# The turn of a deformable-convolution kernel: ScalarE issues half of the box rows and takes the first units in another order

## What is computed

```python
x = x + _L0_conv_ref(_gn(x), ...)      # attention, 8 heads of 48
x = x + _L1_conv_ref(_gn(x), ...)
# inside _L1_conv_ref:
offset = jnp.clip(_conv(x, off_w, off_b), -max_off, max_off)
mask = 2.0 * jax.nn.sigmoid(_conv(x, mask_w, mask_b))
y = _deform_conv(x, offset, mask, proj_w, proj_b)   # 9 taps, bilinear, 384 -> 384
yn = (y - mean) * rsqrt(var + 1e-05) * gamma + beta # mean, var over the batch
return gelu(yn)
```

## Time and profile before

| | |
|---|---|
| median of 3 runs | 3217.5 us (3216.02 to 3220.64) |
| the profiled execution | 3215.74 us |
| its span (first to last instruction) | 3213.9 us |
| PE / DVE / ACT / POOL busy | 2853.9 / 2057.6 / 1638.9 / 900.9 us |
| DMA | 327.84 MB, mean 102 GB/s |

### The profile page before, as it was taken

The page is one execution under the profiler, slowest core; times in us unless marked ns, Lnnn a source line. Parts: engine busy times, 40 slices in busy tenths (PEclk is TensorE's granted clock), DMA queues, the critical chain, the costliest instruction groups (busy, mean ns, idle before and its releaser), DMA issues.

```text
span 3213.9 us, 80068 instructions
## 1 busy us (share of the span) xinstructions
PE 2853.9 (89%) x32858; PEld 1660.8 (52%) x32858; DVE 2057.6 (64%) x3435; ACT 1638.9 (51%) x2828; POOL 900.9 (28%) x633
## 2 busy tenths in 40 slices
PE   4897999979999799989999799997999989995693
PEld 2454555545555455545555455554555545562461
DVE  5774677746776477855777467674677647773234
ACT  4363544645455553745537354465546555372554
POOL 0351113611153110821127111361116311171110
PEclk9899999989999899999999899998999989997796
DMA  4003551055410652126520455105531065304658
GB/s 143 21 2 104 147 132 57 2 144 150 105 43 22 170 136 78 37 75 159 139 69 3 116 147 128 51 2 146 154 99 42 29 149 135 90 21 164 192 148 326
DMA packets 176190, 327.84 MB, mean 102 GB/s; under 512 B 21036, under 2 KB 101036, under 8 KB 168960
## 3 DMA queue, kind: packets, MB, share of 16 engines
q1 hardware_dynamic: 75760, 182.90, 22.1%
q10 hardware_dynamic: 98400, 126.45, 12.9%
q0 software_dynamic: 1584, 12.58, 0.9%
HBM read 227.58 MB, written 75.27 MB: 94 GB/s over the span
## 4 chain that ended last, share of the span: by engine, by line
PE 38%; issue 20%; POOL 15%; DMA 10%; ACT 6%; DVE 5%; SPq 3%; ACTq 2%; POOLq 0%; DVEq 0%
PE R L1797 14%; POOL PL L810 14%; PE R L1773 7%; PE G L1559 5%; DMA P<-positions_scratch 4%; PE G L1592 3%; DMA hats_scratch<-MHL 3%; PE R L1637 3%; SPq L722 2%; ACTq L1109 2%; PE R L1714 2%; ACT HYB L1081 2%; DVE MXP L1289 1%; DMA positions_scratch<-XP 1%; PE R L1655 1%
## 5 line engine op out<-in xcount | busy, mean ns | idle before, releaser
L1797 PE MATMUL R<-P,WALL 128*128 128x512 f16 x3888 | 937.4, 379 | 7.1 <-issue 7.1
L1289 DVE TENSOR_REDUCE MXP<-G 128x1 f32<-128x512 f32 x997 | 656.2, 686 | 301.4 <-PE G L1592 299.8
L810 POOL TENSOR_TENSOR PL<-P 128x1024 f16<-128x1024 f32 x263 | 600.4, 2288 | 624.8 <-ACT P L989 623.3
L989 ACT ACTIVATE P<-R 128x1024 f32<-128x1024 f32 x512 | 519.6, 1022 | 222.9 <-PE R L1637 222.6
L1797 PEld LDWEIGHTS R<-P,WALL 128*128 128x128 f16 x3888 | 369.5, 97 | 426.5 <-issue 8.1
L1361 DVE TENSOR_TENSOR PL<-P 128x1024 f16<-128x1024 f32 x249 | 457.5, 1842 | 97.9 <-ACT P L989 97.5
L834 POOL TENSOR_TENSOR MHL<-M,MHL 128x504 f16<-128x504 f32 (+1 forms) x144 | 168.1, 1167 | 1114.0 <-ACT MHL L1093 1114.0
L1637 PE MATMUL R<-QK 48*128 48x512 f16 (+1 forms) x3072 | 427.9, 384 | 21.3 <-ACT P L989 12.5
L1655 PEld LDWEIGHTS R<-VS,P 128*128 128x128 bf16 x4096 | 322.7, 97 | 187.4 <-issue 129.6
L1592 PE MATMUL G<-QK,QZ 112*128 112x512 f16 x997 | 378.5, 386 | 22.0 <-DVE MXP L1289 20.0
L1655 PE MATMUL R<-VS,P 128*128 128x49 f16 x4096 | 373.0, 186 | 9.7 <-DVE PL L1361 7.2
(11 more groups left out here) (147 smaller groups left out, 3018.7 us busy)
## 6 DMA issues: line engine op xcount, KB each, us to landing
P<-positions_scratch SPq DMA_DIRECT2D x288, 256.0 KB, 4.3
PM<-positions_scratch SPq DMA_DIRECT2D x144, 256.0 KB, 4.6
XB<-hats_scratch ACTq DMA_DIRECT2D x144, 133.0 KB
XB<-hats_scratch ACTq DMA_DIRECT2D x144, 129.5 KB
XB<-hats_scratch ACTq DMA_DIRECT2D x144, 126.0 KB
hats_scratch<-MHL ACTq DMA_DIRECT2D x48, 266.0 KB
hats_scratch<-MHL ACTq DMA_DIRECT2D x48, 259.0 KB
X<-x SPq DMA_DIRECT2D x8, 1536.0 KB, 7.7
```

The costliest lines, as they stand in the source:

```text
L810: pool.tensor_tensor(PL[:, s % P_BUFS, :], P32[:, s % P_BUFS, :], high_view(s), ALU.subtract).then_inc(p_low_pool, 1)
L989: act.activation(P32[:, s % P_BUFS, :], ST[s % 2], ACT.Exp, scale=SCALE).then_inc(p_exp, 1)
L1289: dve.reduce_max(MXP[:, name[1] % 2, n // 2, n % 2:n % 2 + 1], chunk(sec, name)[:, :], AX.X).then_inc(dve_read, 1)
L1797: last = pe.matmul(R6[:, CT + ct, :], WALL[:, w:w + 128], PHL[:, u % 2, part // 2, t, :], start=(u % TAPS == 0 and n < CT), stop=(u % TAPS ...
```

## The change

- `AHEAD` becomes 2: products and fp16 copies are made two units ahead.
- ACT issues the six box row transfers of q = 2 and 3, right behind the mask; SP issues the other six as before and no longer has any between unit 0's and unit 1's rows.
- ACT's turn is written out anew: after unit 0's fp16 copy it reads one fill and stores unit 0, and the x hats of unit 1 come behind that; then load of unit 0, fill, y hats of unit 1, fill, its fp16 copy, x hats of unit 2, store of unit 1, v piece 5, the copy of the sampled unit 0, load of unit 1, y hats of unit 2. v pieces 3 and 4 stand before and between unit 0's hats.
- DVE reads v pieces 3 and 4 before the first product, three fills before the second, and makes the remainder of the sampled unit 0 before the third.

```diff
-UNIT_COUNT, T_RING, AHEAD = 4, 2, 3
+UNIT_COUNT, T_RING, AHEAD = 4, 2, 2
...
# sync
                 for u in range(UNITS):
                     spread(units_0, out_0, u)
-                    if u == 0:
-                        boxes_out(range(2, PER_BLOCK))
...
# scalar, behind the mask (MSK)
                 act.wait_ge(act_read, sec.at(("comb",), "A"))
+                act.wait_ge(xt_low, b * 16 + 16)
+                for q in (2, 3):
+                    for part, a in ((0, 0), (1, 1), (2, 0)):
+                        act.dma_start(box_rows(q, part), transposed_rows(q, a)).then_inc(xt_in[q], 16)
...
# scalar, taps
+                    def sample_high(u):
+                        act.wait_ge(sampled, m_0 + (u + 1) * UNIT_COUNT)
+                        for t in range(CT):
+                            act.activation(PHL[:, u % 2, 0, t, :], R6[:, t, :], ACT.Copy).then_inc(p_hi, 1)
+                    if not final:
+                        v_halves(3)
                     hats_x(0)
+                    if not final:
+                        v_halves(4)
                     hats_y(0)
                     m_halves(0, 0)
-                    if not final:
-                        v_halves(3)
-                        v_halves(4)
+                    next_fill()
+                    store_m(0, 0)
+                    next_fill()
                     if reach == NEAR_OFF:
                         hats_x(1)
-                    for q in range(PER_BLOCK):
-                        act.wait_ge(xt_in[q], b * 48 + 48)
-                    for n in range(AHEAD):
-                        here, after = [divmod(k, per_unit(reach)) for k in (n, n + 1)]
-                        if n < T_RING:
-                            store_m(*here)
-                        if reach == NEAR_OFF:
-                            if n > 0:
-                                hats_x(n + 1)
-                            hats_y(n + 1)
-                        next_fill()
-                        if n < T_RING:
-                            load_boxes(*here)
-                        if n + 1 < AHEAD:
-                            m_halves(*after)
-                    while fills:
+                        boxes_landed()
+                        load_boxes(0, 0)
                         next_fill()
+                        hats_y(1)
+                        next_fill()
+                        m_halves(1, 0)
+                        hats_x(2)
+                        store_m(1, 0)
+                        if not final:
+                            v_halves(5)
+                        sample_high(0)
+                        load_boxes(1, 0)
+                        hats_y(2)
...
-                            if c == per_unit(reach) - 1:
-                                for t in range(CT):
-                                    act.activation(PHL[:, u % 2, 0, t, :], R6[:, t, :], ACT.Copy).then_inc(p_hi, 1)
+                            if c == per_unit(reach) - 1 and (reach == MAX_OFF or u > 0):
+                                sample_high(u)
...
# vector, taps
-                    products_of_hats(0, 0)
                     if not final:
                         v_lower(3)
                         v_lower(4)
-                    for n in range(1, AHEAD):
-                        next_fill()
-                        products_of_hats(*divmod(n, per_unit(reach)))
-                    while fills:
+                    products_of_hats(0, 0)
+                    for _ in range(TURN_FILLS - 1):
                         next_fill()
+                    products_of_hats(*divmod(1, per_unit(reach)))
+                    next_fill()
+                    if reach == NEAR_OFF:
+                        if not final:
+                            v_lower(5)
+                        sample_low(0)
```

More of the change, by code:

```diff
@@ L610, in windows, with box_rows, transposed_rows @@
             return bass.AP(a.tensor, at, [list(a.ap[0]), [HW, hi - lo], [1, width(reach)]])
+        def box_rows(q, part):
+            return XT[q][part * BOX_PIX:(part + 1) * BOX_PIX, :]
+        def transposed_rows(q, a):
+            return XTN[q * BOX_PIX:(q + 1) * BOX_PIX, a, :, :].rearrange("p j c -> p (j c)")
         def in_rows(a, reach):
@@ L721, in boxes_out @@
                     for part, a in ((0, 0), (1, 1), (2, 0)):
-                        sp.dma_start(XT[q][part * BOX_PIX:(part + 1) * BOX_PIX, :],
-                                     XTN[q * BOX_PIX:(q + 1) * BOX_PIX, a, :, :].rearrange("p j c -> p (j c)")).then_inc(xt_in[q], 16)
+                        sp.dma_start(box_rows(q, part), transposed_rows(q, a)).then_inc(xt_in[q], 16)
             def rows_of_taps(b, final):
@@ L1118, in next_fill, with boxes_landed @@
                             read_chunk(fills.pop(0), sec, b + 1)
+                    def sample_high(u):
+                        act.wait_ge(sampled, m_0 + (u + 1) * UNIT_COUNT)
+                        for t in range(CT):
+                            act.activation(PHL[:, u % 2, 0, t, :], R6[:, t, :], ACT.Copy).then_inc(p_hi, 1)
+                    def boxes_landed():
+                        for q in range(PER_BLOCK):
+                            act.wait_ge(xt_in[q], b * 48 + 48)
+                    if not final:
+                        v_halves(3)
@@ L1145, in taps @@
+                        hats_y(2)
+                    else:
+                        boxes_landed()
+                        load_boxes(0, 0)
+                        next_fill()
+                        next_fill()
+                        m_halves(0, 1)
+                        store_m(0, 1)
+                        load_boxes(0, 1)
                     for u in range(UNITS):
@@ L1152, in taps @@
                                 m_halves(nu, nc)
-                            if not final and u == 0 and c == 0:
+                            if not final and u == 0 and c == 0 and reach == MAX_OFF:
                                 v_halves(5)
@@ L1485, in taps, with sample_low @@
                         v_lower(4)
-                    for n in range(1, AHEAD):
+                    products_of_hats(0, 0)
+                    for _ in range(TURN_FILLS - 1):
                         next_fill()
-                        products_of_hats(*divmod(n, per_unit(reach)))
-                    while fills:
-                        next_fill()
+                    products_of_hats(*divmod(1, per_unit(reach)))
+                    next_fill()
+                    def sample_low(u):
+                        for t in range(CT):
+                            dve.wait_ge(p_hi, p_0 + (u * CT + t + 1))
+                            dve.tensor_tensor(PHL[:, u % 2, 1, t, :], R6[:, t, :], PHL[:, u % 2, 0, t, :],
+                                              ALU.subtract).then_inc(p_lo, 1)
+                    if reach == NEAR_OFF:
+                        if not final:
+                            v_lower(5)
+                        sample_low(0)
                     for u in range(UNITS):
@@ L1509, in taps @@
                             read_chunk(name, sec, b + 1)
[L1510 to L1513, removed]
+                        if reach == MAX_OFF or u > 0:
+                            sample_low(u)
                         for n, name in enumerate(beside(u, not final)):
```

## The result

The changed kernel takes 3187.13 us (median of 6 runs, 3182.68 to 3199.89), the kernel before beside it 3216.76 (6 runs, 3211.78 to 3222.81): ratio 0.9911, 95% interval 0.9891 to 0.9932. The profiled execution took 3182.68 us, its span is 3180.9. Forecast were 3193 and a gain of 24.4 us; 29.6 came, 33.1 between the two profiled executions. The seven turns with fills gained 20 us, where 22.4 were forecast, and the last turn 1 of 2; another 10 us came from units 3 to 17, where nothing was expected.

What follows compares the result with a forecast made beforehand. The taps were taken as bound by PE except in the turn, where PE waits for fill readings delayed on ACT. Seven turns at 3.2 us plus 2 for the last made 24.4 us off, 3193 us median; stated range 3170 to 3215.

Steps and rivals of the forecast that it cites:

- The turn: Each of the seven turns with fills, followed through the sixth batch's: gains 3.2 us.
- the reading: DVE's reading, inside unit 1, of the first fill made after unit 0: at 2231.6 against 2234.81; later readings keep this distance.
- PX: Unit 0's position row, sharing the queues with the box rows moved to ACT: lands 2.7 us later, bounds 0 and 5.5.
- load 0: Load of unit 0, issued once unit 0's store lands: at 2211.9 instead of 2213.20, then PE's releaser for unit 0.
- The wait inside unit 1: PE, after unit 1's first box, stands some 2.7 us until DVE reads a fill.
- the landing of store 0: Time from unit 0's store to its load's issue: 3.46 us because the last box rows have landed; 4.58 the bound.
- Two ahead instead of three: In the loop, stores wait for a split about 1 us later, covered by a whole unit: costed at nothing.
- The last turn: The turn without fills: sampled unit 0's remainder comes earlier, unit 1's load later; gains 2 us, bounds 0 and 5.
- The moved box rows are free: Rival for the turn: ACT's box rows delay no position rows, 5.8 us gained a turn, 3175 us; chance 0.17.
- The position rows go last: Rival for the turn: all 5.5 us of ACT's box rows precede PX, 0.3 us gained a turn, 3213; chance 0.15.
- PE's clock falls in the new wait: Rival for the turn: 10 us of low clock in the full stretch, 1.8 us lost a turn, 3228; chance 0.13.
- The issues on ACT: ACT issues six box transfers at some 0.7 us each, under its wait for PX: costs nothing.

Runs made afterwards that it cites:

- run 1: The kernel before with only the six box row transfers moved to ACT, old order and three ahead kept: 3208.99 us, ratio .9980.
- run 12: The kernel before with six box row transfers on ACT and two products ahead, in the old order: 3192.12 us, ratio .9929.
- run 3: The kernel before with two products ahead in place of three, nothing else: 3199.73 us, ratio .9953.
- run 5: The kernel before, three ahead, with SP sending the rows of the maxima one unit's position rows later: 3207.22 us, ratio .9982.
- run 2: The changed kernel with all twelve box row transfers on SP as before: 3183.00 us, ratio .9899.
- run 4: The changed kernel with unit 2's y hats ahead of the sampled unit 0's copy and unit 1's load: 3158.25 us, ratio .9825.
- run 6: run 4 with ACT's readings of the two fills and two v pieces behind unit 0 moved ahead of unit 2's copy: 3166.05 us, ratio .9848.
- run 7: run 6 with all twelve box row transfers on SP: 3160.93 us, ratio .9838.
- run 8: run 6 with all four maxima readings, in place of two, ahead of product 3 on DVE in unit 1: 3169.39 us, ratio .9855.
- run 9: run 7 with all four maxima readings, in place of two, ahead of product 3 on DVE in unit 1: 3169.03 us, ratio .9852.

## Why the prediction was right, and where it was not

**The turn: right step by step up to the reading, and the total in part by luck.** Sixth turn, after the mask, before to after, with the forecast in brackets: PX 2.5 us later (2.7); product 0 2.2 later (2.6); store 0 0.6 earlier (0.2); load 0 2.3 earlier (1.3, the landing took 2.9 us, not 3.46); unit 0 9.3 earlier (8.4); unit 1 8.7 earlier (7); the reading inside unit 1 at 40.8, 3.1 earlier (3.2). The wait inside unit 1 was 4.5 us and not 2.7, because unit 1 began earlier and the reading did not. Unit 2 comes 2.8 earlier; the mean of the seven turns at unit 3 is 2.9, for 3.2 forecast.

Two terms that nearly cancel stand between the reading and that total. The forecast took over the reading's 3.2 us as the turn's gain. But before, the reading held nobody: it was over at 2235.49 and needed only behind unit 1's first box, at about 2236.5, and PE stood 0.4 us elsewhere in unit 1, which it does not now. By that the turn should have gained 3.1 + 1.0 + 0.4 = 4.5 us. Against it, PE is busy for 15.56 us from unit 1 to unit 2 where 13.80 did before, at a mean clock of 0.83: the lower clock took 1.8 of the 4.5.

One reason that the forecast gives is not borne out. It let the landing of store 0 fall from 4.58 to 3.46 us because the last box rows had landed. With the boxes on ACT and the old order (runs 1 and 12) store 0 to load 0 still took 4.6 and 4.7 us; only both parts together brought it to 3.3.

**"Two ahead instead of three. I cost it at nothing": wrong, the step that failed.** I looked at the store and load, whose cover holds, and not at the other thing that moves by a unit: which PX row ACT wants, and what stands ahead of it on SP. Run 3 gives 15 us for it alone, the last turn's 6.2 among them, and shows 1.5 us a batch between units 3 and 17; run 5 gives 5.7 us to SP's rows of the maxima alone. In the changed kernel units 3 to 17 gained 1.4 us a batch, 10 us in seven.

**The last turn: the size was right by luck.** Forecast 2, measured 0.95 us at unit 17 (202.30 to 201.35). It is a sum of two that I did not see: 6.2 from two ahead (run 3), less 5.5 by the new order (run 12 against the changed kernel). Load 0 stayed near 43 us because of the store's landing, and in the new order the y hats of unit 1 stand behind it.

**The sum.** 7 x 2.9 + 7 x 1.4 + 0.95 = 31 us of the 33.1 between the profiled executions, where I had 24.4. The other 2 lie where nothing was changed: 0.7 ahead of the first mask, 0.5 between unit 17 and the next mask (the fifth batch gained 2.0 there and the seventh lost 1.8), the rest behind the last unit 17. So much two executions differ anyway.

**The rivals.** *The moved box rows are free* fell as a mechanism: PX came 2.0 us later (changed kernel against run 2). But 1.1 us of that comes back where store 0 lands (4.4 us from store 0 to load 0 in run 2, 3.3 in the changed kernel), which I had not counted, so run 2 is no faster that can be told. *The position rows go last* fell too: 2.5, not 5.5 us. *PE's clock falls in the new wait* happened, at about half the size that would have decided: behind the wait the clock was 0.50 for 3.4 us, where 6.4 us of low clock were to decide. It happened in every turn: from unit 1 to unit 2 PE is busy for 15.5 to 16.0 us in the seven, 1.7 to 2.2 over the 13.8 of before (sixth turn), some 13 us in all. Unit 1 to unit 2 took 19.8 us in the mean of the seven turns, where it took 14.2 before; run 4 took 3.1 of the 5.6 back by moving one piece of ACT's work. The issues on ACT cost 3.31 and 2.91 us for three, some 1 us each and not 0.7, but under the wait for PX, as forecast.

## What to carry to other kernels

When a pipeline's depth changes, list everything that moves by a stage, on every queue: the operands asked for earlier or later, and what stands ahead of them on the issuing engine, not only the stage's own cover. When a wait on the bounding engine is removed, look which reading on the same helper engine ends the next one; in most turns of runs 6 to 9 a wait freed was replaced by another, of up to 3.5 us, while filling a helper's own idle time (run 4) kept its gain. When two parts of a change each move the same wait, measure each with and without the other: here neither alone made store 0 land sooner. In the last turn a small store on the path that all wait for stood in a queue behind bulk loads; whether another queue would have helped is not tested.

## What the runs showed of the hardware

After a wait at the same instruction the clock is lower in one turn and not in the next. In run 6 PE stood 2.90 us in the sixth turn and 2.02 us in the seventh, at the same instruction; the stretches behind the two waits:

```profile
2208.00:2212.50 4.50, 4.50 (x13) 2.22 (x14) 1.55 (x3) 2.93 (x7) 1.74 (x2) 0.62 0.94 173
...
2581.28:2584.00 2.72, 2.72 (x13) 1.58 (x14) 0.54 (x1) 1.36 (x4) 0.63 (x1) 1.00 1.04 194
```

Unit 1 to unit 2 takes 18.4 us in the one turn and 15.8 in the other; PE is busy for 15.5 us of the one and 13.8 of the other. The length of the wait alone does not tell: in run 4 the 3.3 us behind a wait of 1.33 us ran at 0.58, and in run 7 the stretch behind a wait of 2.91 us, sixth turn, ran at the full clock:

```profile
2196.95:2203.00 6.05, 6.05 (x28) 3.37 (x29) 3.11 (x6) 4.42 (x10) 1.74 (x2) 1.00 0.76 195
```

Also new to me was the landing of a 252 KB store: 2.9 us in a turn with fills (the changed kernel's sixth), 4.3 with all boxes on SP (run 2's sixth), and in the changed kernel's last turn 18.6 to the load's issue (2934.22 to 2952.77) with nine loads ahead of it on its queue.
